# Another order of DVE, ScalarE and TensorE around the first two head products, and feed-forward weights converted in quarters

## The chip, the cores and the metric

One core of one Trainium2 chip. The time is the device time of one execution in microseconds (us). The kernel before was timed in 3 runs: median 1927.71 us, 1926.1 to 1930.4. TensorE is PE in the profile, VectorE DVE, ScalarE ACT, GpSimd POOL and SyncE SP.

## The reference

Two transformer layers on x of shape (128, 64, 256), fp32, 16 heads of 16, hidden width 1024. Layer 1's norms carry a scale and shift computed from `cond`, its q and k are rotated, and it has a mask over the keys. Reduced to what matters:

```
# layer 0 (layer 1: adaptive norms, rotary on q and k, mask, no gates)
y = layernorm(x) * (1 + gamma1) + beta1
q, k, v = split(y @ qkv_w + qkv_b)
x = x + (softmax(q k^T / 4) v @ proj_w + proj_b) * alpha1
z = layernorm(x) * (1 + gamma2) + beta2
x = x + (gelu(z @ fc1_w + fc1_b) @ fc2_w + fc2_b) * alpha2
```

## The kernel before

The 8192 tokens are 16 tiles of 512; each layer takes the 16 tiles in turn, so there are 32 tiles, and NT is 16. One step `u` of the program does the attention of tile `u`, the feed-forward of tile `u - 1`, the first norm and the q, k, v products of tile `u + 1`, the load and first normalisation of tile `u + 2`, and the output of tile `u - 2`. Each engine has its own `step` function, an order written out by hand (SP L438, POOL L600, ACT L763, PE L1080, DVE L1410); arguments `n, a, b, c, p` are the layers of tiles `u + 2`, `u + 1`, `u`, `u - 1` and `u - 2`, or None. Each engine executes its list strictly in order; between engines there are semaphores. Steps 2 to 13 and 18 to 29 run in loops; -1 to 1, 14 to 17 and 30 to 33 are written out, so that layer changes and special cases stand there.

Every product is done in three passes of fp32r operands, high x high, high x low, low x high (`product`, L886). So each operand has a high part, written by ACT (a copy that rounds), and a low part, the difference: DVE makes it for the heads (`ot_lo`, L1368), y, z and the weights (`wgt_lo`, L1187 and L1191), POOL for the hidden activations (`h_lo`, L551).

A tile has four groups `g` of 128 tokens. For a group: `scores` into bank A, `maximum` and `subtract` on DVE (L1335, L1341), `exponential` on ACT, `turn_probs` and `weigh_values` into bank B, `reciprocals` and `normalise_heads` on DVE, `turn_heads` into bank E (L1047), `high_heads` on ACT (L760), `low_heads` on DVE (L1368), `project` into bank E, then in layer 0 `gate_heads` (L1375), `residual` (L1384), `second_statistics` (L1388) and `second_aggregate` (L1392) on DVE, `second_rstd` on POOL (three small operations, L541 to L545), and `second_norm` on ACT.

The feed-forward of a tile is 8 chunks `m`: `hidden` into bank C (L886), gelu on ACT (L740), `hidden_high` on ACT, `hidden_low` on POOL (L551), `back` into banks D. There are one bank C and two buffers of a chunk, so `hidden(m + 1)` waits for gelu of `m`. POOL's order is `hidden_low(0)`, `second_rstd(u, 0)`, `hidden_low(1)`, `second_rstd(u, 1)`, `hidden_low(2)`; it is not changed.

ACT's exponential and gelu need different tables. A table load stands in the program by itself (ACT_TABLE_LOAD), ahead of the activation that needs it.

Around the first two head products TensorE's order is `turn_heads(0)`, `weigh_values(1, 1)`, `hidden(0)`, `project(0)`, `first_turn` 0 and 1 (transposes of tile u + 1 into A0 and B1, followed on DVE by `y_scale`, `y_shift` and, after ACT, `y_low`), `turn_heads(1)`, `hidden(1)`, `project(1)`, `back(0)`, `hidden(2)`, `back(1)`, `queries_keys(0)`.

Layer 1's weights are converted in place of layer 0's. ACT writes the high and DVE the low part of the whole tensor: QKV in step 15, the output projection in step 16, and both feed-forward matrices (2048 columns each) in step 17, ahead of the first use in the same step.

Of the kernel before, what the change touches and what calls it, by code (L numbers as in the profile page):

```python
# [64 lines left out]
def build(nc, t, out):  # L65

    ctx = ExitStack()
    with ctx:
# [77 lines left out]
        minus_half = sb("minus_half", [P, G])  # L146
        rtab = sb("rtab", [P, 2, S])
# [99 lines left out]
        W_AT = (None, slice(W_PROJ, W_FF1), slice(W_FF1, W_FF2), slice(W_FF2, W_ALL))  # L247

# [68 lines left out]
        def _(sp):  # L317
# [78 lines left out]
            def third():  # L396

                sp.wait_ge(w_lo[2], 1)
# [39 lines left out]
            def step(u, n, a, b, c, p):  # L438
# [32 lines left out]
                if b == 0:  # L471
                    wait_apart(sp, sp_passed, (x1_moved, upto(u, 16, 0)))
                    if known(u) and u == 0:
                        wait_apart(sp, sp_passed, (w_lo[3], 1))
# [176 lines left out]
        def _(act):  # L651
            def high_weights(n, layer):
                act.wait_ge(w_in[n], 16 * ((1, 2, 1, 1)[n] if layer == 0 else (4, 4, 2, 2)[n]))
# [7 lines left out]
            def begin():  # L661
                first_norm(0)
# [5 lines left out]
            def second():  # L668
# [3 lines left out]
                high_weights(2, 0)  # L672
                high_weights(3, 0)
# [62 lines left out]

            def hidden(tile, layer, m):
# [25 lines left out]
            def step(u, n, a, b, c, p):  # L763
# [37 lines left out]
                if known(u) and u == NT + 1:  # L801
                    act.wait_ge(pe_f2, upto(NT, MC, 0))
                    high_weights(3, 1)
# [42 lines left out]
                if a == 0:  # L846
                    high_qk(u + 1, 0, 3)
                if c is not None:
# [16 lines left out]
                if b is not None:  # L865
                    high_heads(u, b, 3)
                if a is not None:
# [13 lines left out]
        def _(pe):  # L881
# [48 lines left out]
            def third():  # L930
# [6 lines left out]
                pe.wait_ge(w_lo[2], 1)  # L937
                pe.wait_ge(w_lo[3], 1)
# [119 lines left out]
            def hidden(tile, m):  # L1058
                if m == 0:
# [526 lines left out]
```

## Time and profile before

| what | us |
|---|---|
| median of 3 runs | 1927.71 |
| run of the profiled execution | 1930.19 |
| span in its profile | 1928.4 |
| PE busy | 1806.2 |
| ACT busy | 1307.8 |
| DVE busy | 1235.5 |
| POOL busy | 849.7 |

The span is that from the first to the last instruction of the profile. Busy times of PE contain overlaps with its weight loads (PEld), and the ends of matmuls are modelled, so starts are the safer figures. A time in brackets behind a row is idle time of the engine before this instruction, with the engine and line that ended it.

### The profile page before, as it was taken

How to read it: one execution, taken by the hardware profiler on the slowest of the kernel's cores; microseconds unless marked ns; L12 is line 12 of the kernel's file. 1: busy time of each engine (PE TensorE's matmuls, PEld its weight loads, DVE VectorE, ACT ScalarE, POOL GpSimd, SP SyncE). 2: the span in 40 equal slices, each digit the busy share in tenths (PEclk: the TensorE clock that was granted, in tenths of full speed). 3: DMA queues.
4: the chain of work that ended last, by engine and by line, in shares of the span. 5: the costliest groups of instructions: out<-in, count | busy, mean ns of one | idle time of the engine just before them, and what ended most of it. 6: DMA issues, size and time to landing. Idle time of an engine off the chain costs nothing.

```text
span 1928.4 us, 41731 instructions
## 1 busy us (share of the span) xinstructions
PE 1806.2 (94%) x12623; PEld 1646.5 (85%) x12623; DVE 1235.5 (64%) x2973; ACT 1307.8 (68%) x2315; POOL 849.7 (44%) x1036
## 2 busy tenths in 40 slices
PE   5779999999999999999897999999999999999997
PEld 4668988888898888889787989999988998998985
DVE  5656666767666676766676567767666766766651
ACT  3347776776777677777666676776676677677663
POOL 2123333343333334334544565555555555556433
PEclk8879999999999999999998999999999999999999
DMA  6464434444443444543343233333323333332320
GB/s 162 110 138 103 102 97 114 120 121 129 104 100 98 111 120 122 128 107 96 109 142 95 73 93 103 97 102 106 92 81 104 97 96 105 110 82 85 98 60 33
DMA packets 330275, 199.84 MB, mean 104 GB/s; under 512 B 160994, under 2 KB 314596, under 8 KB 330212
## 3 DMA queue, kind: packets, MB, share of 16 engines
q1 hardware_dynamic: 330212, 199.06, 38.8%
q8 instruction: 32, 0.52, 0.1%
q14 instruction: 31, 0.25, 0.0%
HBM read 80.98 MB, written 17.33 MB: 51 GB/s over the span
## 4 chain that ended last, share of the span: by engine, by line
PE 66%; DVE 13%; issue 10%; POOL 7%; ACT 2%; DMA 1%; SPq 1%; DVEq 0%; POOLq 0%; ACTq 0%
PE D L886 16%; PE C L886 12%; PE A L886 12%; PE B L1036 7%; PE B L886 7%; PE B L1022 4%; PE E L886 3%; POOL h_lo L551 2%; DVE mx L1335 2%; POOL q_flat L597 2%; DVE o_sb L1359 2%; PE A L1008 2%; DVE exps L1341 1%; DVE ot_lo L1368 1%; PE E L1047 1%
## 5 line engine op out<-in xcount | busy, mean ns | idle before, releaser
L551 POOL TENSOR_TENSOR h_lo<-hact,h_hi 128x512 fp32r<-128x512 f32 x256 | 330.5, 1291 | 325.0 <-ACT h_hi L745 317.0
L886 PE MATMUL D<-wgt_hi,h_hi 128*128 128x256 f32 x1024 | 304.2, 297 | 27.3 <-POOL h_lo L551 18.6
L886 PE MATMUL D<-wgt_lo,h_hi 128*128 128x256 f32 x1024 | 290.7, 284 | 0.0
L886 PE MATMUL D<-wgt_hi,h_lo 128*128 128x256 f32 x1024 | 290.4, 284 | 0.0
L886 PE MATMUL A<-k_pad,q_pad 128*128 128x256 f32 x1536 | 260.9, 297 | 9.8 <-DVE mod L1206 4.7
L740 ACT ACTIVATE hact<-C,b_col 128x512 f32<-128x512 f32 x256 | 176.2, 688 | 124.0 <-PE C L886 121.8
L1036 PE MATMUL B<-v_blocks,probs_turned 128*128 128x68 f32 x2048 | 255.8, 272 | 0.0
L1036 PEld LDWEIGHTS B<-v_blocks,probs_turned 128*128 128x128 f32 x2048 | 250.7, 193 | 5.2 <-ACT probs_turned L754 2.5
L754 ACT COPY probs_turned<-B 128x512 f32<-128x512 f32 x256 | 147.8, 585 | 157.1 <-PE B L1022 157.0
L886 PEld LDWEIGHTS D<-wgt_hi,h_hi 128*128 128x128 f32 x1024 | 196.1, 191 | 44.5 <-POOL h_lo L551 29.8
L886 PEld LDWEIGHTS A<-k_pad,q_pad 128*128 128x128 f32 x1536 | 215.6, 195 | 13.8 <-DVE mod L1206 4.9
L1335 DVE TENSOR_REDUCE mx<-A 128x8 f32<-128x512 f32 x256 | 174.3, 681 | 79.2 <-PE A L1008 48.6
L886 PE MATMUL C<-z_hi,wgt_hi 128*128 128x512 f32 x512 | 210.6, 411 | 6.1 <-ACT hact L740 4.7
L749 ACT ACTIVATE exps<-exps 128x512 f32<-128x512 f32 x256 | 161.2, 630 | 79.7 <-DVE exps L1341 79.0
L886 PE MATMUL C<-z_hi,wgt_lo 128*128 128x512 f32 x512 | 201.1, 393 | 0.0
L886 PE MATMUL C<-z_lo,wgt_hi 128*128 128x512 f32 x512 | 200.5, 392 | 0.0
L886 PEld LDWEIGHTS D<-wgt_hi,h_lo 128*128 128x128 f32 x1024 | 196.7, 192 | 1.3
L886 PEld LDWEIGHTS D<-wgt_lo,h_hi 128*128 128x128 f32 x1024 | 196.3, 192 | 0.0
L1341 DVE TENSOR_TENSOR exps<-A,mx 128x512 f32<-128x512 f32 x256 | 173.9, 679 | 3.8 <-PE B L1022 0.5
L541 POOL TENSOR_SCALAR rs<-mv 128x1 f32<-128x1 f32 x128 | 30.0, 234 | 323.8 <-DVE mv L1392 321.2
L1022 PE MATMUL B<-ident,exps 128*128 128x128 f32 x1024 | 157.3, 277 | 8.4 <-DVE o_sb L1359 5.2
L1359 DVE TENSOR_TENSOR o_sb<-B,rden 64x128 f32<-64x128 f32 x512 | 146.5, 286 | 24.9 <-PE E L1047 7.7
(138 smaller groups left out, 4231.5 us busy)
## 6 DMA issues: line engine op xcount, KB each, us to landing
k_pad<-k_flat SPq DMA_DIRECT2D x512, 64.0 KB, 2.1
q_pad<-q_flat SPq DMA_DIRECT2D x256, 128.0 KB, 2.3
gates<-gates SPq DMA_DIRECT2D x64, 256.0 KB, 4.5
x_bias<-x_bias SPq DMA_DIRECT2D x32, 512.0 KB, 3.5
rotation<-rotation SPq DMA_DIRECT2D x256, 64.0 KB, 1.9
x_in<-in_x SPq DMA_DIRECT2D x16, 512.0 KB, 4.2
gates<-gated_bias SPq DMA_DIRECT2D x32, 256.0 KB, 4.9
x_res<-in_x SPq DMA_DIRECT2D x16, 512.0 KB, 4.2
```

Source lines behind the costliest of these rows:

```text
L551: pool.tensor_tensor(hb[1][:, m % 2, :], hact[:, m % 2, :], hb[0][:, m % 2, :].bitcast(F32), ALU.subtract).then_inc(h_lo, 1)
L597: pool.tensor_tensor(flat[keys][:, :, i % KC, 1, :], by_group(rot_sum[:, i % KC, :]), flat[keys][:, :, i % KC, 0, :].bitcast(F32), ALU.sub ...
L740: nc.scalar.activation(hact[:, m % 2, :], C[:, :], ACT.Gelu, bias=b1_col[:, layer, m:m + 1]).then_inc(gelu, 1)
L749: nc.scalar.activation(exps[:, b, :], exps[:, b, :], ACT.Exp, scale=SCORE_SCALE).then_inc(s_exp, 1)
L754: nc.scalar.copy(pt[:, b, :], B[b][:, :]).then_inc(pt_moved, 1)
L886: ins = nc.tensor.matmul(dst, l, r, start=first_start and n == 0, stop=last_stop and n == len(todo) - 1, **kw)
L1008: ins = nc.tensor.matmul(dst, mean_w[:, :], row, start=False, stop=True)
L1022: ins = nc.tensor.transpose(B[b][:, n * P:(n + 1) * P], exps[:, b, n * P:(n + 1) * P], ident[:, :])
L1036: ins = nc.tensor.matmul(B[b][:, n * 68:(n + 1) * 68], pt[:, b, n * P:(n + 1) * P], moving, start=True, stop=True)
L1335: nc.vector.tensor_reduce(mx[:, b, :], A[b][:, :].rearrange("p (h k) -> p h k", k=S), AX.X, ALU.max)\
L1341: nc.vector.tensor_tensor(exps[:, b, :].rearrange("p (h k) -> p h k", k=S), A[b][:, :].rearrange("p (h k) -> p h k", k=S), mx[:, b, :].rea ...
L1359: ins = nc.vector.tensor_tensor(o_sb[p, b, :].rearrange("p (n j d) -> p n j d", n=4, j=2), sums_of(b)[p, :, x, :, 0:HD], rden[p, b, :].rea ...
```

## The change

- DVE: after `reciprocals(1, 0)` come at once `normalise_heads(1, 0)` and `low_heads(0)`; `maximum(2, 0)` and `(2, 1)` and `subtract(2, 0)` come behind. `low_heads(1)` and `subtract(2, 1)` stand ahead of `y_scale(0)`. `gate_heads(1)` and `residual(1)` stand behind `y_low(0)` and `y_low(1)`.
- TensorE: `hidden(1)` directly behind `project(0)`, then `turn_heads(1)`, the two `first_turn`, `back(0)`, `project(1)`.
- ACT: a gelu of one column (`table_probe`) behind `high_heads(0)`; chunk 0's copy ahead of `high_heads(1)`; both exponentials of group 2 ahead of `second_norm(1)`.
- Weights: the feed-forward matrices in quarters on ACT (`high_piece`) and DVE (`low_piece`), in layer 0's prologue and in steps 16 and 17; those who read them wait for the quarters they need. QKV goes from the middle of step 15 to the end of step 14.

```diff
@@ scalar
+            def high_piece(n, layer, q):
+                act.wait_ge(w_in[n], 16 * (1 + layer))
+                if layer == 1 and n == 2:
+                    act.wait_ge(pe_f1, upto(NT - 1, MC, 2 * q + 2))
+                elif layer == 1:
+                    act.wait_ge(pe_f2, upto(NT - 1, MC, 2 * q + 2))
+                nc.scalar.copy(ff_piece(n, wgt[0][:, W_AT[n]], q), ff_piece(n, w_source(n, layer), q)).then_inc(w_hi[n], 1)
+            def gelu_table():
+                nc.scalar.activation(table_probe[:, :], minus_half[:, 0:1], ACT.Gelu)
...
                 if known(u) and u == NT + 1:
-                    act.wait_ge(pe_f1, upto(NT, MC, 0))
-                    high_weights(2, 1)
+                    high_piece(2, 1, 3)
+                    high_piece(3, 1, 2)
...
                     high_heads(u, b, 0)
-                if known(u) and u == NT - 1:
-                    act.wait_ge(pe_v, upto(NT, 2, 0))
-                    high_weights(0, 1)
+                if c is not None:
+                    gelu_table()
+                if known(u) and u == NT + 1:
+                    high_piece(3, 1, 3)
                 if c is not None:
                     hidden(u - 1, c, 0)
+                if c is not None:
+                    hidden_high(u - 1, 0)
                 if b is not None:
                     high_heads(u, b, 1)
-                if c is not None:
-                    hidden_high(u - 1, 0)
...
                     exponential(u, 2, 0)
+                    exponential(u, 2, 1)
                     second_norm(u, 1)
-                    exponential(u, 2, 1)
...
+                if known(u) and u == NT:
+                    high_piece(2, 1, 0)
+                    high_piece(2, 1, 1)
                 if c is not None:
                     hidden(u - 1, c, 4)
...
+                if known(u) and u == NT - 2:
+                    act.wait_ge(pe_v, upto(NT, 2, 0))
+                    high_weights(0, 1)
+                if known(u) and u == NT:
+                    high_piece(3, 1, 1)
+                    high_piece(2, 1, 2)
                 if n is not None:
                     first_norm(u + 2)
@@ tensor
                     project(u, 0)
+                if c is not None:
+                    hidden(u - 1, 1)
+                if b is not None:
+                    turn_heads(u, 1, c)
                 if a is not None:
                     first_turn(u + 1, 0, b)
                     first_turn(u + 1, 1, b)
-                if b is not None:
-                    turn_heads(u, 1, c)
-                if c is not None:
-                    hidden(u - 1, 1)
+                if c is not None:
+                    back(u - 1, 0)
                 if b is not None:
                     project(u, 1)
                 if c is not None:
-                    back(u - 1, 0)
                     hidden(u - 1, 2)
                     back(u - 1, 1)
@@ vector
+            def low_piece(n, layer, q):
+                dve.wait_ge(w_hi[n], 4 * layer + q + 1)
+                nc.vector.tensor_tensor(ff_piece(n, wgt[1][:, W_AT[n]], q), ff_piece(n, w_source(n, layer), q),
+                                        ff_piece(n, wgt[0][:, W_AT[n]], q).bitcast(F32), ALU.subtract).then_inc(w_lo[n], 1)
...
                     reciprocals(u, 1, 0)
-                    maximum(u, 2, 0)
                     normalise_heads(u, 1, 0)
-                    maximum(u, 2, 1)
                     low_heads(u, b, 0)
                     reciprocals(u, 1, 1)
-                    subtract(u, 2, 0)
+                    maximum(u, 2, 0)
                     normalise_heads(u, 1, 1)
                 if b == 0:
                     gate_heads(u, 0)
                 if b is not None:
                     residual(u, b, 0)
+                    subtract(u, 2, 0)
+                    maximum(u, 2, 1)
+                    second_statistics(u, 0)
+                if b is not None:
+                    low_heads(u, b, 1)
                     subtract(u, 2, 1)
-                    second_statistics(u, 0)
-                if known(u) and u == NT - 1:
-                    low_weights(0, 1)
                 if a is not None:
                     y_scale(u + 1, 0)
                 if b is not None:
                     second_aggregate(u, 0)
-                    low_heads(u, b, 1)
                 if a is not None:
                     y_shift(u + 1, 0)
                     y_scale(u + 1, 1)
+                    y_shift(u + 1, 1)
+                    y_low(u + 1, 0)
                 if b == 0:
                     gate_heads(u, 1)
                 if a is not None:
-                    y_shift(u + 1, 1)
+                    y_low(u + 1, 1)
                 if b is not None:
                     residual(u, b, 1)
-                if a is not None:
-                    y_low(u + 1, 0)
-                if b is not None:
                     second_statistics(u, 1)
-                if a is not None:
-                    y_low(u + 1, 1)
-                if b is not None:
                     second_aggregate(u, 1)
                 if known(u) and u == NT + 1:
-                    low_weights(3, 1)
+                    low_piece(2, 1, 3)
+                    low_piece(3, 1, 2)
+                    low_piece(3, 1, 3)
...
+                if known(u) and u == NT - 2:
+                    low_weights(0, 1)
+                if known(u) and u == NT:
+                    low_piece(2, 1, 0)
+                    low_piece(2, 1, 1)
+                    low_piece(3, 1, 0)
+                    low_piece(3, 1, 1)
+                    low_piece(2, 1, 2)
```

## Rows read from the trace of the kernel before

**Rows 1.** Steps 8, 15, 17, 23: us, busy PE, PEld, DVE, ACT, POOL, PEclk, DMA.

```profile
511.17:567.36 56.19, 54.44 (x387) 49.45 (x386) 37.55 (x92) 40.81 (x73) 20.85 (x27) 1.00 0.44 113
904.74:968.36 63.62, 57.24 (x387) 52.42 (x385) 43.00 (x101) 42.59 (x78) 31.87 (x39) 0.95 0.44 116
...
1028.08:1098.90 70.82, 59.88 (x403) 55.32 (x402) 43.34 (x94) 44.23 (x74) 33.55 (x39) 0.90 0.28 79
1382.53:1439.22 56.69, 55.65 (x402) 51.32 (x401) 37.77 (x90) 40.38 (x73) 31.70 (x39) 1.00 0.34 97
```

**Rows 2.** TensorE's waits: us in total, times, longest.

```profile
PE E L886 <- DVE ot_lo L1368: 27.0, 36, 3.4
PE D L886 <- POOL h_lo L551: 18.6, 38, 1.8
```

**Rows 3.** Timeline of layer 0, step 8: start us, duration, instruction.

```profile
524.51 0.48 PE L886 MATMUL C<-z_hi,wgt_hi 128*128 128x512 f32 x1
...
526.31 0.61 DVE L1368 SCALAR_TENSOR_TENSOR ot_lo<-E,v_bias,ot_hi 128x128 fp32r<-128x128 f32 x2
...
527.07 0.36 PE L886 MATMUL E<-wgt_hi,ot_hi 128*128 128x256 f32 x1 [0.91 <-DVE ot_lo L1368]
...
535.18 0.28 PE L886 MATMUL D<-wgt_hi,h_hi 128*128 128x256 f32 x1
```

**Rows 4.** DVE's timeline in the same step, behind `project(0)`.

```profile
528.15 0.43 DVE L1375 TENSOR_TENSOR E<-E,gates 128x256 f32<-128x256 f32 x1
...
529.05 0.68 DVE L1341 TENSOR_TENSOR exps<-A,mx 128x512 f32<-128x512 f32 x1
529.65 0.42 DVE L1388 BATCH_NORM_STATS2 st<-x_res 128x6 f32<-128x256 f32 x1
529.98 0.68 DVE L1271 TENSOR_TENSOR A<-A,mod_tile 128x512 f32<-128x512 f32 x1
530.57 0.17 DVE L1392 BATCH_NORM_AGGREGATE mv<-st 128x2 f32<-128x6 f32 x1
```

**Rows 5.** Timeline of layer 1, step 23, all engines.

```profile
1395.38 0.38 PE L1047 MATMUL E<-ident,o_sb 128*128 128x128 f32 x2
...
1395.80 0.63 ACT L760 ACTIVATE ot_hi<-E,v_bias 128x128 fp32r<-128x128 f32 x2 [0.58 <-PE E L1047]
...
1396.41 0.48 PE L886 MATMUL C<-z_hi,wgt_hi 128*128 128x512 f32 x1
...
1397.90 0.35 PE L886 MATMUL E<-wgt_hi,ot_hi 128*128 128x256 f32 x1
...
1398.15 1.28 ACT L740 ACT_TABLE_LOAD   x1 [1.72 <-PE C L886]
1399.44 0.69 ACT L740 ACTIVATE hact<-C,b_col 128x512 f32<-128x512 f32 x1
...
1400.18 0.50 PE L886 MATMUL C<-z_hi,wgt_hi 128*128 128x512 f32 x1 [0.24 <-ACT hact L740]
...
1402.61 0.22 POOL L541 TENSOR_SCALAR rs<-mv 128x1 f32<-128x1 f32 x1
...
1403.92 1.30 POOL L551 TENSOR_TENSOR h_lo<-hact,h_hi 128x512 fp32r<-128x512 f32 x1
...
1405.57 0.28 PE L886 MATMUL D<-wgt_hi,h_hi 128*128 128x256 f32 x1
```

**Rows 6.** The same step: aggregate of group 1 on DVE, and POOL behind it.

```profile
1405.77 0.17 DVE L1392 BATCH_NORM_AGGREGATE mv<-st 128x2 f32<-128x6 f32 x1
...
1406.29 0.22 POOL L541 TENSOR_SCALAR rs<-mv 128x1 f32<-128x1 f32 x1 [1.07 <-DVE mv L1392]
```

**Rows 7.** Step 17: the feed-forward weights on ACT and DVE, POOL beside them.

```profile
1034.33 1.90 ACT L659 CAST wgt_hi<-w_raw 128x2048 fp32r<-128x2048 f32 x1
...
1058.62 2.26 DVE L1191 TENSOR_TENSOR wgt_lo<-gates,wgt_hi 128x2048 fp32r<-128x2048 f32 x1
...
1058.99 1.96 POOL L541 TENSOR_SCALAR rs<-mv 128x1 f32<-128x1 f32 x1 [1.14 <-DVE mv L1392]
```

More of the change, by code:

```diff
@@ L146, in build @@
         minus_half = sb("minus_half", [P, G])
+        table_probe = sb("table_probe", [P, 1])
         rtab = sb("rtab", [P, 2, S])
@@ L247, in build, with ff_piece @@
         W_AT = (None, slice(W_PROJ, W_FF1), slice(W_FF1, W_FF2), slice(W_FF2, W_ALL))
+        def ff_piece(n, region, q):
+            if n == 2:
+                return region.rearrange("p (k n) -> p k n", k=KC)[:, :, 2 * q * P:2 * (q + 1) * P]
+            return region[:, 2 * q * D:2 * (q + 1) * D]
         def w_source(n, layer):
@@ L396, in third @@
             def third():
-                sp.wait_ge(w_lo[2], 1)
+                sp.wait_ge(w_lo[2], 4)
                 for n in range(2):
@@ L651, in _ @@
         def _(act):
+            def high_piece(n, layer, q):
[5 more added lines that the diff above has]
+                nc.scalar.copy(ff_piece(n, wgt[0][:, W_AT[n]], q), ff_piece(n, w_source(n, layer), q)).then_inc(w_hi[n], 1)
             def high_weights(n, layer):
-                act.wait_ge(w_in[n], 16 * ((1, 2, 1, 1)[n] if layer == 0 else (4, 4, 2, 2)[n]))
+                act.wait_ge(w_in[n], 16 * ((1, 2)[n] if layer == 0 else 4))
                 if n == 0:
@@ L661, in begin @@
             def begin():
+                act.wait_ge(sem_ident, 3)
                 first_norm(0)
@@ L671, in second @@
                 nc.scalar.activation(hact[:, 1, :], C[:, :], ACT.Tanh).then_inc(gates_tanh, 1)
-                high_weights(2, 0)
-                high_weights(3, 0)
+                for n in (2, 3):
+                    for q in range(MC // 2):
+                        high_piece(n, 0, q)
                 act.wait_ge(mod_done, 16)
@@ L866, in step @@
                     high_heads(u, b, 3)
+                if known(u) and u == NT:
+                    high_piece(3, 1, 0)
                 if a is not None:
@@ L936, in third @@
                 pe.wait_ge(gates_tanh, 1)
-                pe.wait_ge(w_lo[2], 1)
-                pe.wait_ge(w_lo[3], 1)
+                pe.wait_ge(w_lo[2], 4)
+                pe.wait_ge(w_lo[3], 4)
             def first_turn(tile, pair, attn):
@@ L1058, in hidden @@
             def hidden(tile, m):
+                if known(tile) and tile == NT and m % 2 == 0:
+                    pe.wait_ge(w_lo[2], 4 + m // 2 + 1)
                 if m == 0:
-                    if known(tile) and tile == NT:
-                        pe.wait_ge(w_lo[2], 2)
                     pe.wait_ge(z_hi, upto(tile, 2, 2))
@@ L1068, in back @@
             def back(tile, m):
+                if known(tile) and tile == NT and m % 2 == 0:
+                    pe.wait_ge(w_lo[3], 4 + m // 2 + 1)
                 if m == 0:
-                    if known(tile) and tile == NT:
-                        pe.wait_ge(w_lo[3], 2)
                     await_(pe, f2_read, upto(tile, 2, 0))
@@ L1243, in second @@
                 nc.vector.tensor_copy(maskT[:, :], E[:, 0:P]).then_inc(mask_turned, 1)
-                low_weights(2, 0)
-                low_weights(3, 0)
+                for n in (2, 3):
+                    for q in range(MC // 2):
+                        low_piece(n, 0, q)
                 dve.wait_ge(rows_out, 80)
@@ L1426, in step @@
                     low_weights(1, 1)
-                if known(u) and u == NT + 1:
-                    low_weights(2, 1)
                 if b is not None:
@@ L1544, in step @@
                     second_aggregate(u, 3)
+                if known(u) and u == NT - 2:
+                    low_weights(0, 1)
+                if known(u) and u == NT:
+                    low_piece(2, 1, 0)
[3 more added lines that the diff above has]
+                    low_piece(2, 1, 2)
             program(dve, begin, second, third, step)
```

5 lines of the change are left out of this document (1 added, 4 removed).

## The prediction

> **What bounds the kernel now.** I read the windows by step first. A step of layer 0 takes 56.19 us, one of layer 1 56.69 us, and TensorE is busy in 54.4 and 55.7 us of them while ACT, DVE and POOL are busy in no more than 41 of them [rows 1]. So TensorE's order sets the time, and only the places where it waits can give anything. Two steps stick out, both at the change of layers: step 15 with 63.62 and step 17 with 70.82 us, at a granted clock of 0.95 and 0.90 [rows 1]. Next the list of waits: `project` (bank E) waits 27.0 us in all for DVE's `ot_lo`, and `back` (bank D) 18.6 us for POOL's `h_lo` [rows 2]. Last the timeline around chunk 0's product in one step of each layer; I call the start of `hidden(0)` on TensorE H. H is 524.51 in layer 0 and 1396.41 in layer 1 [rows 3, 5], and the changed stretch ends with `back(1)`, which starts at H+10.67 in layer 0 and at H+9.16 in layer 1 [rows 3, 5]. Behind `back(1)` TensorE's order is untouched, so the change of this offset is what a step gains or loses.
>
> **DVE's low heads ahead of the maxima.** `project(0)` could start at H+1.49, as it does in layer 1, but in layer 0 waits until H+2.56 because `ot_lo` starts at 526.31 and ends 0.15 us ahead of it [rows 3, 5]. Two operations on 512 columns, at 0.60 us from start to start [rows 4], leave the place before it, so `ot_lo` starts near 525.1, ends near 525.8 and `project(0)` starts at H+1.49: 1.07 us earlier in layer 0, nothing in layer 1.
>
> **The gelu table.** In layer 1 the load of 1.28 us starts at H+1.74, when chunk 0 is there, gelu follows at once with 0.69 us, and TensorE's `hidden(1)` starts at H+3.77 [rows 5]. The probe has no wait on TensorE, stands right behind `high_heads(0)`, which ends at 1396.43, and its load ends at about 1397.7, ahead of H+1.74. Gelu then starts at H+1.74 and `hidden(1)`, now directly behind `project(0)`, at H+1.74+0.69+0.05 = H+2.48. The probe itself is one element wide and lies in the 0.4 us that are left. The Trainium skill (ScalarE: Activation LUTs, What ACT_TABLE_LOAD costs) gives 2.66 us for a switch, a drain of 1.38 us behind the 1.28 us of the load. The rows show 1.29 us from the load's start to gelu's, and no drain. By the page gelu would come at H+2.7 instead of H+1.74 and everything summed below 0.95 us later in each of 27 steps, 26 us more and slower than before; since the row has both ends of a load in it, I give this no chance of its own.
>
> **What is late next.** `turn_heads(1)` follows at T = H+2.48+1.49 = H+3.97; group 0's residual, which it also waits for, is there (`gate_heads` starts 1.08 us behind `project(0)`, the next subtraction 0.90 us behind that [rows 3, 4], so about H+3.5). The transposes of the next tile, `back(0)`, `project(1)` and `hidden(2)` would bring TensorE to `back(1)` near H+8.8 (0.2 + 0.9 + 1.5 + 0.8 + 1.4 us). But `back(1)` needs POOL's `h_lo(1)`, and on POOL `second_rstd(0)` stands ahead of it, which waits for DVE's `second_aggregate(0)`. Today this is hidden: only `stats` and `y_scale` lie between the subtraction and the aggregate (0.60 + 0.33 + 0.59 [rows 4]). In the new order DVE has `low_heads(1)` and `subtract(2,1)` there too, and `low_heads(1)` waits for `turn_heads(1)` on TensorE and `high_heads(1)` on ACT. Step by step from T: ACT starts 0.42 later and takes 0.63 [rows 5], DVE starts at T+1.07; `low_heads` 0.53 (0.61 less the overlap of 0.08 that 0.68 against 0.60 shows [rows 3, 4]), `subtract` 0.60, `y_scale` 0.59, aggregate 0.17 [rows 4]; POOL starts 0.35 behind its end [rows 6]; from there to `h_lo(1)` 1.31, `h_lo(1)` 1.30 [rows 5], and 0.15 to TensorE as above. That is T+6.07, `back(1)` at H+10.04, with TensorE idle for some 1.2 us. So the stall of `project` is handed to `back(1)`.
> Layer 0: 10.67 - 10.04 = 0.63 us gained a step, steps 1 to 14: -8.8 us. Layer 1: 9.16 - 10.04 = 0.88 us lost a step, steps 18 to 30: +11.4 us. Bounds of the price of this chain: if no link of it binds, `back(1)` is at H+8.8, 1.9 gained in layer 0 and 0.4 in layer 1; upwards each link may be 0.1 late, H+10.5.
> Further back `second_norm(1)` now stands behind both exponentials on ACT, and DVE's aggregate of group 1 behind both `y_low`. I find `h_lo(2)` 0.15 us ahead of `back(2)`: no price, but no room either.
>
> **Weights, step 15.** 7.4 us over its neighbours [rows 1]. The QKV weights' 1536 columns stand between the head products there: by ACT's 1.90 and DVE's 2.26 us for 2048 [rows 7] that is 1.4 + 1.7 = 3.1 us, and a clock of 0.95 over 63.6 us costs up to 3.2 more. I take 4.9 between these; the rest belongs to POOL's first rotation and stays. The weights now stand at the end of step 14, where ACT has no idle time: and five copies, 1.4 us by the same row and up to 1.9 for being five, delay `first_norm`, the last gelu and `exponential(0,0)`. I take 1.9: net -3.0, bounds -5 to 0.
> **Step 17.** 14.1 us over a step of layer 1 [rows 1]: twice ACT's 1.90 and DVE's 2.26 in a row [rows 7], each with TensorE waiting behind it, then the low clock. Now quarters of 0.57 us on DVE and 0.48 on ACT. At the end of step 16 two of ACT's (1.0 us) and five of DVE's (2.9 us) stand ahead of the next `exponential` and `maximum`; in step 17 three of DVE's stand ahead of the sines, in idle time of about 2 us. And POOL: `rs`, 0.22 us else [rows 5], took 1.96 us beside DVE's subtraction of 2.26 us, and ended with it [rows 7]. So POOL's second norms and `h_lo` come later by the quarters they meet. I put 1.2 us for the end of step 16, 1.0 for the middle of step 17, and 0.9 for the chain above: net -11.0, bounds -14 to -6.
> The Trainium skill says the same of the port (SBUF — State Buffer, SBUF: two separate sides): a DVE operation with two SBUF inputs and a GpSimd operation that reads SBUF exclude each other for the whole instruction. The trace agrees, with those 1.96 us. By that rule every quarter that meets POOL's chain is paid in full, which is the rival P.
> Begin: eight quarters for two whole subtractions, up to 0.3 us more. Steps 16, 31 and 32: nothing, bounds -2 to +1. SP waits for counts of 4 in the place of 1, met at the same time; its queue does not move.
>
> **Sum.** -8.8 + 11.4 - 3.0 - 11.0 + 0.3 = -11.1 us on the profiled span of 1928.4. Its run took 1930.19, the median of the others is 1927.71; against the median the change gives 1916.6, and I say 1917.
>
> **Rivals.**
> B, the chain does not bind: `second_rstd(0)` is early enough, and the stalls go as the change intends. Then 14 x 1.9 + 13 x 0.4 = 31.8 and 14.0 + 0.9 - 0.3 at the transition: 1881. For it: the chain has seven handovers, and more of it may overlap than the rows of another order show. Against it: it would have to be 1.2 us shorter than its measured pieces. 0.08.
> C, slower: `back(2)`. `second_norm(1)` behind both exponentials and the later aggregate makes `h_lo(2)` late. The place is `back(2)`, behind the chain aggregate, POOL, ACT, POOL; it costs from 0.15 us of lateness on, and 0.6 us beyond that in 27 steps are 16 us more: 1933. It makes the whole slower from 0.4 us beyond the slack on. For it: no row shows this order, and each link adds its error. Against it: ACT's move of the exponential also brings it forward. 0.12.
> P, the port: quarters and POOL exclude each other one by one, and the transition gains a third of what I say: 1917 + 9 = 1926. 0.12.
> The forecast, within a few us: 0.68.
>
> **Range and chances.** The forecast's own bounds are 0.25 us in 27 steps and 4 at the transition: 1909 to 1925. To leave out no more than B and half of C the range goes to 1906 and 1927. Within 0.2% of the old time is 1923.9 to 1931.6, about what a measurement can tell from no change. Faster: all of B, 0.6 of the forecast's 0.68, a little of P: 0.72. Same: 0.17. Slower: 0.11.
>
> **What will show it.** Right: `project(0)` without idle time in both layers; `hidden(1)` at H+2.5; `back(1)` waits over 1 us for `h_lo` in every step, and the waits of D for `h_lo` rise from 18.6 to over 50 us while those of E for `ot_lo` fall to below 5; steps of layer 0 near 55.6 us, of layer 1 near 57.6, step 17 near 60. Wrong: layer 1 at or below 56.3 (B), `back(2)` with a wait of its own (C), step 17 above 64 (P).

## The result and the profile after

| | before | changed |
|---|---|---|
| median, us (15 runs each) | 1927.71 (1924.98 to 1932.67) | 1923.39 (1921.17 to 1925.29) |
| profiled execution: its time, its span | 1930.19, 1928.4 | 1921.17, 1919.4 |
| step of layer 0 (step 8) | 56.18 | 55.73 |
| step of layer 1 (step 23) | 56.72 | 57.61 |
| step 15 / 17 / 18 | 63.87 / 70.82 / 56.77 | 62.56 / 58.41 / 59.62 |

The ratio is 0.9976 (0.9968 to 0.9983): 4.3 us faster, where I had said 10.7. (A step runs here from one `second_turn(0)` to the next.) The two profiled executions differ by 9.0 us, the medians by 4.3, since one stands 2.5 us above its kernel's median and the other 2.2 below.

The windows of steps 8, 15, 17, 18 and 23 of the changed kernel answer to [rows 1]; columns: window, us, busy time of PE, PEld, DVE, ACT and POOL with their instructions, granted clock, DMA share, GB/s.

```profile
506.97:562.70 55.73, 54.42 (x386) 49.55 (x385) 37.90 (x92) 41.09 (x74) 20.78 (x27) 1.00 0.44 113
896.83:959.39 62.56, 56.31 (x388) 51.43 (x387) 45.11 (x101) 43.00 (x80) 33.41 (x40) 0.97 0.46 119
1018.53:1076.94 58.41, 55.92 (x402) 51.48 (x401) 40.87 (x96) 42.48 (x77) 33.49 (x41) 1.00 0.35 95
1076.94:1136.56 59.62, 55.61 (x403) 51.39 (x402) 38.01 (x90) 40.83 (x74) 31.64 (x39) 1.00 0.33 94
1367.10:1424.71 57.61, 55.60 (x402) 51.38 (x401) 38.02 (x90) 40.81 (x74) 31.67 (x39) 1.00 0.34 96
```

Layer 0 gains, layer 1 loses more, step 17 gives 12.4 us, and step 18, of which I had said nothing, costs 2.0 more than its successors. TensorE's waits (us in total, times, longest) have changed places against [rows 2]: 27.0 us for `ot_lo` have become 1.4, and 18.6 us for `h_lo` have become 56.0.

```profile
PE D L916 <- POOL h_lo L558: 56.0, 73, 2.3
PE E L916 <- DVE ot_lo L1405: 1.4, 3, 0.6
```

Where these waits are is in the timeline of step 8, which answers to [rows 3 to 5]:

```profile
520.31 0.48 PE L916 MATMUL C<-z_hi,wgt_hi 128*128 128x512 f32 x1
520.33 1.28 ACT L756 ACT_TABLE_LOAD   x1
521.03 0.61 DVE L1405 SCALAR_TENSOR_TENSOR ot_lo<-E,v_bias,ot_hi 128x128 fp32r<-128x128 f32 x2
521.79 0.35 PE L916 MATMUL E<-wgt_hi,ot_hi 128*128 128x256 f32 x1
522.07 0.69 ACT L761 ACTIVATE hact<-C,b_col 128x512 f32<-128x512 f32 x1 [0.24 <-PE C L916]
522.80 0.50 PE L916 MATMUL C<-z_hi,wgt_hi 128*128 128x512 f32 x1
524.29 0.38 PE L1077 MATMUL E<-ident,o_sb 128*128 128x128 f32 x2
...
525.37 0.61 DVE L1405 SCALAR_TENSOR_TENSOR ot_lo<-E,v_bias,ot_hi 128x128 fp32r<-128x128 f32 x2
...
527.09 0.17 DVE L1429 BATCH_NORM_AGGREGATE mv<-st 128x2 f32<-128x6 f32 x1
...
527.61 0.22 POOL L548 TENSOR_SCALAR rs<-mv 128x1 f32<-128x1 f32 x1 [2.85 <-DVE mv L1429]
...
528.91 1.27 POOL L558 TENSOR_TENSOR h_lo<-hact,h_hi 128x512 fp32r<-128x512 f32 x1
530.23 0.39 PE L916 MATMUL D<-wgt_hi,h_hi 128*128 128x256 f32 x1 [1.10 <-POOL h_lo L558]
```

H is 520.31. `project(0)` starts at H+1.48, `hidden(1)` at H+2.49, `turn_heads(1)` at H+3.98, all without idle time; then DVE's aggregate waits its turn behind `ot_lo` and a subtraction, POOL stands 2.85 us still for it, and `back(1)` starts at H+9.92, 1.10 us late. In step 23 it is H+9.92 too. This is the handed-over stall of the forecast.

### The profile page after: what moved, and what is told of

Its sections match the earlier page's. It is cut to its first block, busy times and chain, and to the rows that moved or that the text cites. A ratio compares the mean times of both kernels' runs of the same rounds, so it can differ in the third digit from the quotient of the medians.

```text
span 1919.4 us, 41799 instructions
## 1 busy us (share of the span) xinstructions
PE 1795.0 (94%) x12623; PEld 1639.3 (85%) x12623; DVE 1247.6 (65%) x2985; ACT 1318.5 (69%) x2359; POOL 848.4 (44%) x1036
## 4 chain that ended last, share of the span: by engine, by line
PE 57%; DVE 12%; POOL 11%; issue 11%; SPq 3%; ACT 2%; DMA 1%; POOLq 1%; DVEq 1%; ACTq 0%
PE D L916 14%; PE A L916 11%; PE C L916 9%; PE B L1066 8%; PE B L916 7%; POOL h_lo L558 5%; PE B L1052 4%; SPq L328 2%; DVE exps L1378 2%; POOL q_flat L604 2%; DVE mx L1372 2%; PE A L1038 2%; DVE o_sb L1396 1%; POOL rs L550 1%; PE E L916 1%
## 5 line engine op out<-in xcount | busy, mean ns | idle before, releaser
L766 ACT CAST h_hi<-hact 128x512 fp32r<-128x512 f32 x256 | 159.3, 622 | 5.2
```

The source lines that it names most:

```text
L766: nc.scalar.copy(hb[0][:, m % 2, :], hact[:, m % 2, :]).then_inc(h_hi, 1)
```

## Experiments

Each run is compared with the kernel before, on the same chip; "to before" is the ratio of times with its interval. Step times are of the profiled executions.

**The two parts apart.** First all of the order within the steps, with the weights whole as before (DVE's part of the diff against the changed kernel; on ACT the copies go back to before's places):

```diff
                     low_heads(u, b, 1)
                     subtract(u, 2, 1)
+                if known(u) and u == NT - 1:
+                    low_weights(0, 1)
+                if known(u) and u == NT + 1:
+                    low_weights(3, 1)
...
-                    low_piece(2, 1, 3)
-                    low_piece(3, 1, 2)
-                    low_piece(3, 1, 3)
```

> The changed order of the steps alone: DVE's, ACT's and TensorE's order and the gelu probe as in the changed kernel, the weights of layer 1 in whole copies as before (one place differs: DVE's subtraction for the second matrix of the feed forward stands directly behind group 1's low heads). Theory of the handed-over stall (back(1) now waits for h_lo behind second_rstd(0)): layer 0 gains 0.5 us in each of 14 steps, layer 1 loses 0.9 in each of 13, and the steps 15 to 18 keep their old length plus about 1 us each for the same wait: 5 to 7 us slower than before, near 1933. Rival, my forecast's own terms (0.63 gained, 0.88 lost, nothing at the change of layers): 2.6 us slower, 1930. Rival, the order costs nothing and the changed kernel lost its time at the change of layers alone: at or below 1928.

Measured: 1928.98, to before 1.0009 (1.0000 to 1.0018), 1.1 us slower. Layer 0's steps 55.72, layer 1's 57.61, as in the changed kernel. Step 15 took 60.88, step 17 68.76 (its wait for `wgt_lo` is 3.95 us; before, with the subtraction in the later place, 6.08), step 18 57.67. So the theory's terms for the steady steps hold, but the whole lies below the 5 to 7 us slower that I expected, between the two rivals (1930 and 1928): steps 15 to 17 together came out 5.6 us shorter than in before's profile instead of longer. 2.1 of them are step 17, where DVE's subtraction stands earlier. Then the weights alone, in before's order:

```diff
+                if known(u) and u == NT - 2:
+                    low_weights(0, 1)
+                if known(u) and u == NT:
+                    low_piece(2, 1, 0)
...
```

> The weights part alone: quarters of the feed forward weights and the QKV weights at the end of step 14 as in the changed kernel, every engine's order within a step as before. Theory that the two parts add: step 17 shrinks by 12 to 13 us, step 15 by 1 to 2 (its first stall stays, since DVE's last copy of the QKV weights still meets POOL's addition of 1024 columns): 1914 to 1916, and the layers' other steps at 56.2 and 56.7 us. Rival, the two parts need each other (the quarters fit only where the new order leaves room): step 17 stays above 62 us and the whole is at 1920 or more. If step 18 is also 2 us or more over its neighbours, its late exchange of rotated rows comes with the weights part; if not, it comes with the order or with one execution.

Measured: 1920.62, to before 0.9966 (0.9954 to 0.9978), 7.3 us faster and not 13. The whole is where the rival had it (1920 or more), but not for the rival's reason: step 17 gave its whole gain (57.64, 13.2 less), so the parts don't need each other. Step 15 kept its length (63.43), step 18 grew by 1.7 (58.50), and step 31, untouched, took 51.81 for 50.24. In the last TensorE's waits are the same in both (1.2 us for `h_lo` at most), and only here the granted clock is low behind them, 0.97 against 1.00.

**Step 15.** The five QKV copies back in step 15, and on DVE their subtractions behind `subtract(2,1)`:

```diff
+                if known(u) and u == NT - 1:
+                    act.wait_ge(pe_v, upto(NT, 2, 0))
+                    high_weights(0, 1)
                 if c is not None:
                     gelu_table()
```

> The changed kernel with the five QKV copies of layer 1 (ACT) and their subtractions (DVE) back in step 15, between the head products as before. Theory from the order-alone run, whose step 15 took 60.88 us against 62.56 in the changed kernel: moving these copies to the end of step 14 cost more than it saved; here step 15 takes 60.9, step 14 stays at 55.5, the whole is 1.7 us faster than the changed kernel, near 1921.7. Rival: the two step 15s differ only because the profiled runs had the low clock at different places; then this run has a step 15 of 62 to 63 and the whole stays at 1923.4.

Measured: 1919.54, to before 0.9957 (0.9941 to 0.9974); the changed kernel's 0.9976 lies just outside the interval, and the two intervals overlap, so a gain of some 4 us over it is likely but not sure. The profiled execution, at 1922.78 the slowest of the four, does not show where it would be. Step 15 took 62.48 in it, by my expectation the rival's value; its waits are those of the order-alone run to 0.1 us (4.7 for `h_lo`, 1.5 for gelu), which took 60.88. The window of step 15 with the order alone, then in this run:

```profile
897.56:958.44 60.88, 54.58 (x388) 49.84 (x387) 42.39 (x101) 42.83 (x80) 32.57 (x40) 1.00 0.48 123
```

```profile
898.45:960.93 62.48, 56.19 (x388) 51.07 (x387) 42.39 (x101) 42.94 (x80) 32.55 (x40) 0.97 0.47 120
```

Same instructions, same waits, 1.6 us apart, and the granted clock is what differs. So a step of 60.88 against one of 62.56 does not show that moving the copies cost more than it saved: the clock alone makes that much. Whether the old place is better stays open. The move did not shorten TensorE's waits in step 15: they sum to 6.2 us before, in the changed kernel and in this run. Next, what the 3.0 us wait at the start of the changed step 15 is. In the changed kernel DVE's five subtractions by their source line (duration in ns, min/median/max), and then the timeline behind them:

```profile
L1218 DVE TENSOR_TENSOR wgt_lo<-w_raw,wgt_hi x5: 418/693/2597, 896.2 to 898.9; 128x256 fp32r<-128x256 f32 x4, 128x512 fp32r<-128x512 f32 x1
```

```profile
898.65 2.55 POOL L569 TENSOR_TENSOR x_bias<-x_bias,x_res 128x1024 f32<-128x1024 f32 x1
...
901.41 0.68 DVE L1372 TENSOR_REDUCE mx<-A 128x8 f32<-128x512 f32 x1
...
903.43 0.50 PE L916 MATMUL A<-k_pad,q_pad 128*128 128x256 f32 x1 [3.00 <-DVE exps L1378]
```

The last subtraction (256 columns) starts at 898.89, 0.24 behind POOL's addition, takes 2.60 us where its shortest sister took 0.42, and ends 0.28 behind POOL's end; the first maximum of the step stands behind it. The test moves POOL's addition:

```diff
-                if c is not None:
+                late = known(u) and u == NT - 1
+                if c is not None and not late:
                     x1_bias(u - 1, c)
                 if p is not None:
                     hidden_low(u - 2, MC - 1)
+                if late:
+                    x1_bias(u - 1, c)
```

> The changed kernel with one edit on POOL in step 15 alone: its addition of 1024 columns (x1_bias) behind the last h_lo of the tile before, in the place of ahead of it. Theory, contention: DVE's last QKV subtraction (256 columns, 2.60 us in the changed kernel, its shortest sister 0.42) stood still for as long as POOL's addition ran beside it; without that neighbour it takes about 0.4 us, TensorE's wait for the first exponentials of step 15 falls from 3.0 to below 1.0, step 15 from 62.6 to about 60.5. Rival: the five copies are late in themselves (ACT's copies, the sum of DVE's 2.7 us ahead of the last one): the wait stays above 2.5 us. Rival: the late addition gives the two microseconds back later in step 15.

Measured: 1920.12, to before 0.9964 (0.9949 to 0.9978), step 15 59.49 for 62.56. The same views, and the window of the step:

```profile
L1221 DVE TENSOR_TENSOR wgt_lo<-w_raw,wgt_hi x5: 415/421/1503, 898.5 to 901.2; 128x256 fp32r<-128x256 f32 x4, 128x512 fp32r<-128x512 f32 x1
```

```profile
903.52 0.95 PE L919 MATMUL A<-k_pad,q_pad 128*128 128x256 f32 x6 [0.81 <-DVE exps L1381]
```

```profile
899.11:958.60 59.49, 55.29 (x388) 49.92 (x387) 42.77 (x101) 43.02 (x80) 33.17 (x40) 1.00 0.47 126
```

The wait fell from 3.00 to 0.81. One subtraction still takes 1.50, beside POOL's `h_lo`, which takes 1.46 for its usual 1.28, and it too ends 0.28 behind POOL's end: the same between these two. One moved POOL operation took the subtraction from 2.60 to 0.42, so the contention is shown. The low clock goes with the long wait: the eight profiles whose step 15 starts with the 3.0 us wait have 0.95 or 0.97 in it and take 62.6 to 64.1 us, the three with POOL's addition late 1.00 and 58.6 to 59.5.

**Step 18.** TensorE waits 2.26 us for `h_lo` here, which stands on POOL behind a rotation that waits for an exchange of rotated rows. The exchanges for the queries (issue to landing) and the timeline behind them, first two fences in the changed kernel, the next two in before:

```profile
DMA to landing us min/median/max: 1.9/1.9/3.9
```

```profile
1124.25 1.26 POOL L598 TENSOR_TENSOR rotation<-rotation 128x512 f32<-128x512 f32 x1 [2.17 <-DMA rotation<-rotation]
1125.47 1.27 POOL L558 TENSOR_TENSOR h_lo<-hact,h_hi 128x512 fp32r<-128x512 f32 x1
...
1126.79 0.38 PE L916 MATMUL D<-wgt_hi,h_hi 128*128 128x256 f32 x1 [2.26 <-POOL h_lo L558]
```

```profile
DMA to landing us min/median/max: 1.7/1.9/1.9
```

```profile
1143.32 1.30 POOL L591 TENSOR_TENSOR rotation<-rotation 128x512 f32<-128x512 f32 x1 [0.17 <-DMA rotation<-rotation]
```

In windows of 0.25 us the DMA queue of instructions has one transfer of 16 KB near the exchange: before at 44.5 us into the step, 0.1 us behind POOL's rotation at 44.4, so the exchange had landed; order alone at 45.5, rotation at 45.3; changed at 44.5, where the exchange would have let the rotation go at 45.3; weights alone 43.5 against 44.4. So with the weights in pieces the fetch comes about 1 us earlier against the exchange. It is so in every profile of these kernels: in the two without pieces the fetch starts 2.2 and 2.5 us behind the issue of the last exchange, which takes 1.9; in eleven of the twelve with pieces it starts 1.1 to 1.9 behind, and that exchange takes 3.6 to 3.9 (the twelfth is the second run below). Two runs moved it with waits that are met anyway. First in TensorE's first lines:

```diff
+                for _ in range(24):
+                    pe.wait_ge(cond_in, 16)
```

> The changed kernel with 24 more waits on a semaphore that is already there, in TensorE's first lines, where it waits for its first load anyway: nothing of the work changes, only where TensorE's later instructions lie. Step 18 of the changed kernel, of the weights-alone run and of the run with the earlier aggregate is 1.7 to 2.0 us too long: one exchange of rotated rows takes 3.9 us for its usual 1.9, with a transfer of 16 KB of instructions between its rows; before and order alone the same fetch comes some tenths later and hits nothing. Theory, code fetch: the fetch moves with the added instructions, the exchange takes 1.9 us, step 18 takes 57.6. Rival: the exchange is late for what the weights' pieces do themselves: step 18 stays at 59.6. If the fetch doesn't move against the exchange, the run says nothing of it. The whole within 2 us of the changed kernel.

Measured: 1923.38, to before 0.9981 (0.9971 to 0.9990), step 18 59.57, and the fetch still at 44.5: the run says nothing of the delay, only that 24 instructions ahead of the loop don't move this fetch. Then close ahead of step 18:

```diff
+                if known(u) and NT - 1 <= u <= NT + 1:
+                    for _ in range(16):
+                        pe.wait_ge(cond_in, 16)
                 if c is not None:
                     back(u - 1, 1)
```

> The changed kernel with 16 more waits on a semaphore that is already there on TensorE ahead of back(1) in each of the steps 15, 16 and 17, where TensorE waits for h_lo anyway. The 24 waits in TensorE's first lines left the fetch of 16 KB of instructions at the same place in step 18 (44.5 us into it), so if it is TensorE's code its place counts from the end of the loop. Theory, code fetch: 48 instructions more, at some 800 a step of 57 us, bring it about 3 us nearer to the step's start, ahead of the exchanges of rotated rows for the queries; they take 1.9 us each and step 18 takes 57.6 in the place of 59.6. Rival: the exchange is late for another reason: step 18 stays at 59.6 with the fetch elsewhere. Rival: the fetch is not TensorE's: it stays at 44.5 and the run says nothing.

Measured: 1921.73, to before 0.9961 (0.9948 to 0.9975). The fetch came at 43.0, 1.5 us earlier and not 3. The DMA queue of instructions in the 0.25 us from 43.0 (transfers, MB, share of the engines), the exchanges, and the window of step 18:

```profile
q8 instruction: 1, 0.02, 35.1%
```

```profile
DMA to landing us min/median/max: 1.9/2.6/3.0
```

```profile
1078.29:1136.93 58.64, 55.63 (x403) 51.42 (x401) 38.00 (x90) 40.86 (x74) 31.71 (x39) 1.00 0.33 95
```

The fetch now starts ahead of the last exchange; this one took 2.9 and the one before it 3.0, instead of 3.9 and 1.9, and step 18 lost half of its excess (58.64). The exchanges were issued at the same places in the step, the fetch moved with TensorE's code alone, and the delay moved with the fetch; so it is a fetch of TensorE's code, and it delays the exchange. That rests on one run. Half a miss in size: the fetch was not moved clear of all four exchanges. (Step 15 took 64.12 there, at a clock of 0.95 for 0.97.)

**The steady steps.** What the probe is worth:

```diff
-                if c is not None:
-                    gelu_table()
```

> The changed kernel without the probe that asks for the gelu table. Theory: the load of 1.28 us again starts when chunk 0 of the hidden product is there, gelu, hidden(1), turn_heads(1) and the whole chain to back(1) come 1.2 to 1.3 us later in each step: about 30 steps, 35 us slower than the changed kernel, near 1958. Rival: in layer 0, where project(0) and the new order leave more room, half of it is hidden: 1940. Rival, the probe does nothing (its load is not early either): 1923.

Measured: 1952.67, to before 1.0133 (1.0117 to 1.0148), 29 us over the changed kernel for the 35 expected; steps 56.98 and 58.91, 1.25 and 1.30 more. The load stands again behind the product, and TensorE waits for it in each steady step (timeline of step 23, then the list of waits):

```profile
1403.71 1.28 ACT L761 ACT_TABLE_LOAD   x1 [1.72 <-PE C L914]
1405.01 0.69 ACT L761 ACTIVATE hact<-C,b_col 128x512 f32<-128x512 f32 x1
```

```profile
PE C L914 <- ACT hact L761: 35.4, 28, 1.4
```

The miss in size is in the count: steps 14 to 17 and 30 lost next to nothing.

Now the chain to `back(1)`: the aggregate ahead of `low_heads(1)`.

```diff
                     subtract(u, 2, 0)
-                    maximum(u, 2, 1)
                     second_statistics(u, 0)
-                if b is not None:
+                    maximum(u, 2, 1)
+                    second_aggregate(u, 0)
                     low_heads(u, b, 1)
                     subtract(u, 2, 1)
```

> The changed kernel with one edit on DVE: group 0's second statistics directly behind subtract(2,0), and its aggregate behind maximum(2,1), ahead of low_heads(1), subtract(2,1) and y_scale(0). Theory of the chain (back(1) waits 1.2 us in every step because POOL's second_rstd(0) waits for that aggregate): the wait of back(1) goes, back(1) starts at H+8.8 (H is the start of hidden(0)), 1.2 us less in 28 to 30 steps, 34 us faster than the changed kernel, near 1890. Rival, another link is right behind it (h_lo(1) itself behind gelu(1), or ACT): half, near 1907. Rival, POOL's place and not the aggregate makes h_lo(1) late: 1923, with the same wait.

Measured: 1916.32, to before 0.9943 (0.9929 to 0.9956): 6 to 7 us below the changed kernel, where I had expected 34, and less than the first rival's half. Steps 55.67 (0.06 less) and 57.19 (0.42 less). That it is less is the first rival's mechanism, another link right behind: `back(1)` no longer waits; what waits is `back(2)` (timeline of step 8):

```profile
532.41 1.16 ACT L770 ACTIVATE exps<-exps 128x512 f32<-128x512 f32 x2
...
533.08 0.22 POOL L548 TENSOR_SCALAR rs<-mv 128x1 f32<-128x1 f32 x1 [4.05 <-DVE mv L1429]
...
534.52 0.60 ACT L706 ACTIVATE zn<-x_res,nb,rs 128x256 f32<-128x256 f32 x1 [0.96 <-POOL nb L552]
535.03 0.60 ACT L766 CAST h_hi<-hact 128x512 fp32r<-128x512 f32 x1
...
535.72 1.28 POOL L558 TENSOR_TENSOR h_lo<-hact,h_hi 128x512 fp32r<-128x512 f32 x1 [1.29 <-ACT h_hi L766]
537.05 0.39 PE L916 MATMUL D<-wgt_hi,h_hi 128*128 128x256 f32 x1 [0.25 <-POOL h_lo L558]
```

That is the place that the prediction's rival C names: ACT holds `hidden_high(2)` behind `second_norm(1)`, which waits for POOL, and that for DVE's aggregate of group 1, now behind both `y_low`. All of it was hidden behind the late `back(1)`. One edit more, on ACT:

```diff
+                if c is not None:
+                    hidden_high(u - 1, 2)
                 if b is not None:
                     exponential(u, 2, 0)
                     exponential(u, 2, 1)
                     second_norm(u, 1)
-                if c is not None:
-                    hidden_high(u - 1, 2)
```

> The kernel with the earlier aggregate of group 0, and one more edit on ACT: hidden_high(2) (the high half of chunk 2) directly behind its gelu, ahead of both exponentials of group 2 and of second_norm(1). Theory: with back(1) on time the bound is now back(2), whose h_lo(2) waits for hidden_high(2) behind second_norm(1), which waits for POOL and DVE's late aggregate of group 1; ahead of it h_lo(2) is ready 1.3 us earlier and back(2) starts some 0.8 us earlier in layer 0 (step 54.9 in the place of 55.67) and 0.8 in layer 1 (56.4 for 57.18): 24 us less, near 1893. Rival: the exponentials of group 2, 0.6 us later, delay turn_probs(2) by as much as is gained, and steps stay within 0.2 us: 1916. Rival in between: DVE's y_low(1) and POOL's second_rstd(1) ahead of h_lo(2) leave 0.3 us a step: 1907.

Measured: 1900.77, to before 0.9864 (0.9848 to 0.9881), 8 us above the expected 1893. `h_hi(2)` is cast directly behind its gelu, `h_lo(2)` is there in time, and `back(2)` starts without a wait (the same step):

```profile
527.89 0.62 ACT L766 CAST h_hi<-hact 128x512 fp32r<-128x512 f32 x1
...
531.15 1.29 POOL L558 TENSOR_TENSOR h_lo<-hact,h_hi 128x512 fp32r<-128x512 f32 x1
533.31 0.36 PE L916 MATMUL D<-wgt_hi,h_hi 128*128 128x256 f32 x1
```

Steps 55.13 and 56.65, 0.6 and 1.0 below the changed kernel (54.9 and 56.4 expected). And this edit alone, on the changed kernel:

> The changed kernel with hidden_high(2) ahead of the exponentials of group 2 alone, the aggregate where the change has it. Theory, two waits in a row: the earlier aggregate alone gave 0.05 us a step in layer 0 and 0.43 in layer 1, since back(2)'s h_lo(2) came next; with back(1) still late for second_rstd(0), bringing h_lo(2) forward alone gives next to nothing: steps at 55.7 and 57.6, 1923. Rival: it gives the gain of 0.5 us a step by itself, and the aggregate was the lesser half: 1908.

Measured: 1918.85, to before 0.9950 (0.9934 to 0.9965), 5 us below the changed kernel for the nothing expected, though the steps, 55.55 and 57.62, account for 2 us only. Together the two edits take 0.60 us from a step of layer 0, apart 0.06 and 0.18; from one of layer 1 0.96, apart 0.42 and nothing. Two waits in a row: whoever takes one away sees the other.

**All together.** With the late `x1_bias`, and `y_low(1)` ahead of `gate_heads(1)` on DVE, since TensorE waits 0.36 us for `y_lo` in layer 0:

```diff
-                if b == 0:
-                    gate_heads(u, 1)
                 if a is not None:
                     y_low(u + 1, 1)
+                if b == 0:
+                    gate_heads(u, 1)
```

> The three edits that helped, together, and one more: the earlier aggregate of group 0, hidden_high(2) ahead of the exponentials of group 2, x1_bias behind the last h_lo in step 15; and on DVE y_low(1) ahead of gate_heads(1) (layer 0 alone has the latter), since TensorE now waits 0.36 us for y_lo in layer 0. Theory: step 15 takes 60.3 for 63.5 (-3.1), layer 0's steps 0.1 to 0.2 less (-2): 1895.5, against 1900.8 without the two last edits. Rival: the residual of group 1, later by y_low(1), makes its norms and h_lo late, so that layer 0's steps stay or grow: 1898.

Measured: 1900.57, to before 0.9852 (0.9839 to 0.9866). Step 15 fell to 58.73, and layer 0's steps grew from 55.13 to 55.43, as the rival had it, though the whole is above its 1898 too. The norms of group 1 come 0.3 us later, as the rival says, but TensorE doesn't wait for `h_lo`: ACT's `second_norm(1)` and, behind it, its copy of the turned probabilities come 0.3 us later, and `weigh_values(2)` waits for that copy, 8.4 us in all where the same kernel without the swap has 1.1 (timeline of step 8):

```profile
538.98 2.08 PE L1069 MATMUL B<-v_blocks,probs_turned 128*128 128x68 f32 x16 [0.52 <-ACT probs_turned L778]
```

Without that swap:

> The run with all edits without y_low(1) ahead of gate_heads(1): so the earlier aggregate of group 0, hidden_high(2) ahead of the exponentials of group 2, and x1_bias behind the last h_lo in step 15. Theory: the swap of y_low and gate_heads cost 0.30 us in each of 13 steps of layer 0 (55.43 for 55.13); without it layer 0's steps take 55.1 again, step 15 takes 59 us as with all edits: 3.9 us faster than with all edits, near 1896.7. Rival: part of step 15's gain with all edits was the swap's; then step 15 takes 60 or more and the whole is at 1898 to 1899.

Measured: 1895.39, to before 0.9831 (0.9818 to 0.9845): 32 us faster than before, the fastest kernel here, and 1.3 below what I expected. Its steps 7, 15 and 18:

```profile
448.09:503.17 55.08, 54.56 (x386) 49.68 (x385) 37.73 (x92) 41.21 (x74) 20.72 (x27) 1.00 0.46 116
888.77:947.33 58.56, 55.26 (x389) 50.09 (x388) 42.76 (x101) 43.16 (x80) 33.13 (x40) 1.00 0.49 128
1062.91:1122.35 59.44, 56.88 (x402) 53.03 (x401) 38.14 (x90) 40.65 (x74) 30.96 (x38) 0.97 0.34 94
```

TensorE is busy in 54.6 of 55.1 us. Step 18's fetch is still in it: the last exchange takes 3.9 us, and the clock is 0.97 behind the wait, so that this step is 2.8 us over its neighbours.

## Why the prediction was right in its mechanism and wrong in its sum

**Right.** The starts at H+1.49, H+2.48 and H+3.97 came at H+1.48, H+2.49 and H+3.98; the link by link chain to `back(1)` gave H+10.04, measured H+9.92 in both layers. The waits for `h_lo` rose above 50 us and those for `ot_lo` fell below 5, as said. Rival B is out (layer 1 is not at 56.3), rival C did not come to pass, but only because the chain ahead of it was the longer one. From the probe's load at 520.33 to gelu at 522.07 are 1.74 us, and gelu waited for the product at the end; so the drain that the Trainium skill adds to a load (ScalarE: Activation LUTs, What ACT_TABLE_LOAD costs) doesn't show here; nor does it on either side of 93 of before's 185 loads, which start within 0.05 us of the end of what ran ahead of them and are followed within 0.05 us of their own end.

**The profiled sum, term by term** (forecast, then the two profiled executions):

- Start and step 1: -0.3, measured -1.8.
- Layer 0, steps 2 to 14: -8.2, measured -5.9. `back(1)` came 0.75 us earlier in the step, more than the 0.63 said, but only 0.45 was left at the end. What failed here is "behind `back(1)` TensorE's order is untouched, so the change of this offset is what a step gains": 0.10 us went at once in `back(1)`, whose second product starts 0.22 us behind the first instead of 0.12, and 0.24 in `weigh_values(2)`. There TensorE arrives 0.65 us earlier, but ACT's copies of the turned probabilities come only 0.28 earlier. That they set this place is read from the times; in the run of all edits together it shows as a wait.
- Layer 1, steps 18 to 30: +11.4, measured +13.7. Steps 19 to 29 lost 0.92 each for 0.88 said, which is in part luck: `back(1)` came only 0.76 later, and 0.11 more went in its first products, a loss that the prediction did not have. The rest is step 18's 2.0 of the instruction fetch, which I had not looked for.
- Step 15: -3.0, measured -1.3. I took 4.9 for what went and 1.9 for what came. TensorE's waits did not shrink at all (6.2 us before and after); the 1.3 are no more than the clock's 0.95 and 0.97. What came was 3.0 of waiting at the first scores and the low clock behind it, because DVE's last subtraction stood for POOL's addition. That is rival P's mechanism, with the engines in the other roles: I had looked for POOL waiting for DVE, at the quarters, and not for DVE waiting for POOL at the QKV copies, whose place has a POOL operation of 2.4 us right beside it in every step.
- Step 16: 0, measured -0.6. Step 17: -11.0, measured -12.4. Here P bit little: beside the quarters at the end of step 16 POOL's three small operations took 0.37, 0.86 and 1.22, some 1.4 us over their usual length (the last below), and step 17 still came out below 60.

```profile
1017.40 1.22 POOL L552 TENSOR_SCALAR nb<-mv,rs 128x1 f32<-128x1 f32 x1 [0.21 <-POOL rs L550]
```

- Steps 31 and 32: 0, measured -0.8.

That makes -9.0 against -11.1.

**Why the medians moved by 4.3 only.** The forecast for the median, 1916.6, missed 1923.39 by 6.8 us. 2.1 of them are the terms above. 2.5 come from setting a sum made from one execution against the median: that execution of before stood 2.5 us above its median, and I did not ask in which steps. The last 2.2 are chance, since the changed kernel's profiled execution stands 2.2 below its own median.

The step of the prediction that failed is therefore the term of the weights, -3.0 for step 15 and -11.0 for step 17, read from one execution as if it were the usual one. Without the order's chain my terms for them (-3.0, -11.9, +0.3) sum to 14.6; the weights alone gave 7.3 us. In the profile of that run steps 15 to 17 gave 13.6, nearly all of it in step 17; 1.7 went to step 18's exchange and 1.6 to a low clock in step 31; and the two medians lie 2.8 us nearer to each other than the two profiled executions. The order alone cost 1.1 us (0 to 3.5) where my terms for it sum to 2.6.

The clock has its part in this. The low clock of before's profile lay in steps 15 and 17 (0.95 and 0.90 in [rows 1]), just those whose shortening I counted, and of step 15's 7.4 us I booked 1.8 (4.9 less the 3.1 of the copies) as clock that would go. It went in part only: step 15 has 0.95 or 0.97 in each of the eight profiles in which it starts with the 3.0 us wait. Nor is it fixed by the program: with the same waits step 15 takes 60.88 or 62.48, step 31 50.24 or 51.81. In step 17 it did go: 0.90 and 0.93 with whole copies, 1.00 in the twelve profiles with pieces. Before's profiled execution was an unlucky one: over the whole kernel its clock is 0.980, and none of the 49 executions of before that were timed beside the runs has less (0.980 to 0.987, median 0.983; the twelve below 1926 us 0.983 to 0.987, the five above 1930 us 0.981 to 0.983). In which steps they are higher is not recorded, so whether before's usual step 15 or 17 is shorter than the profile's stays open. So does what sets the first 175 us: the start of step 2 lies between 171.4 and 175.1 in the profiles of the changed kernel and its variants, with no edit that would explain it.

## What to carry to other kernels

When a stall is handed on, follow the whole chain at every place at which TensorE waits afterwards, and remove the links together: by their ratios the two edits gave 22 us together, and 6 and 5 apart. Before a sum from one profile is set against a median, look in which stages that execution lies above it, and count a low clock as gained only if a wait that you remove stands ahead of it, and allow that it comes and goes even then. Before copies on DVE are put into a "free" place, look at what POOL does there, since either of the two can be held up by the other (POOL's `rs` in [rows 7], DVE's subtraction in step 15).

## What the runs showed of the hardware

- A DVE subtraction of 256 columns with two SBUF inputs took 2.60 us beside a POOL addition of 2.55, and 0.42 without it; it ended 0.28 us behind POOL's end, as another did beside POOL's `h_lo`; moved apart, the wait behind it fell from 3.00 to 0.81 us. The Trainium skill has this (SBUF — State Buffer, SBUF: two separate sides) as an exclusion for the whole instruction, and the runs agree, with DVE as the one that waits.
- A fetch of 16 KB of instructions that started 1.1 to 1.9 us behind the issue of an exchange of 64 KB made it take 3.6 to 3.9 us instead of 1.9 (eleven profiles), and 2.0 us of it reached TensorE in the changed kernel. 48 more waits in TensorE's code moved the fetch by 1.5 us; 24 ahead of the loop did not move it. In the changed kernel the steps written out have three or four such fetches each and some of 8 KB, steps 3 to 13 and 19 to 29 none.
- Behind the same waits of TensorE (the longest 3.0 us in step 15, 1.2 in step 31) the granted clock fell to its lower level for a while in one execution and not in another, and the step was 1.6 us longer each time.
